# Four engines get orders of their own for the last five pairs of an attention pipeline, and two items' low parts move to VectorE

## What is computed

```
q, k, v = x @ Wq, ctx @ Wk, ctx @ Wv          # 16 heads of 64
logits  = q @ k^T * 64**-0.5 + column_bias
out     = softmax(logits) @ v                 # 128 x 1024
x       = out @ Wo + bo + x
```

## Time and profile before

| | |
|---|---|
| median of three runs | 1821.68 us |
| profiled execution: time / span | 1819.41 / 1816.8 us |
| TensorE matmul busy | 1757.9 us, 97% of the span |
| VectorE, ScalarE, GpSimd busy | 1579.0, 1471.8, 1599.6 us |
| mean granted TensorE clock | 0.978 |

### The profile page before, as it was taken

One profiled execution on the slowest core, in us unless ns is written; L12 is line 12 of the kernel. 1 busy time (PEld: TensorE's weight loads), 2 busy tenths in 40 slices (PEclk: granted clock), 3 DMA queues, 4 the chain that ended last, 5 costly groups with the idle time before them and its releaser, 6 DMA issues.

```text
span 1816.8 us, 72896 instructions
## 1 busy us (share of the span) xinstructions
PE 1757.9 (97%) x28400; PEld 1508.9 (83%) x28400; DVE 1579.0 (87%) x3010; ACT 1471.8 (81%) x2987; POOL 1599.6 (88%) x2136
## 2 busy tenths in 40 slices
PE   5599999999999999999999999999999999999996
PEld 5578888888888888888888888888888888888885
DVE  6689988899889998899888998899888898889983
ACT  3388888888888888888888888888888888888873
POOL 3389999999999999999999998999999999999983
PEclk7599999999999999999999999999999999999997
DMA  5269999999999999999999999999999999989996
GB/s 173 43 133 190 175 180 192 185 185 171 190 185 185 183 172 186 192 182 183 175 186 188 177 189 179 186 188 173 187 185 185 184 178 182 173 171 187 174 184 135
DMA packets 1168210, 320.35 MB, mean 176 GB/s; under 512 B 1140246, under 2 KB 1164124, under 8 KB 1167868
## 3 DMA queue, kind: packets, MB, share of 16 engines
q1 hardware_dynamic: 1167868, 315.69, 94.1%
HBM read 15.93 MB, written 4.19 MB: 11 GB/s over the span
## 4 chain that ended last, share of the span: by engine, by line
PE 90%; issue 1%; DMA 1%; SPq 1%; ACT 0%; DVE 0%; ACTq 0%; DVEq 0%
PE ring L1226 50%; PE sc L1368 12%; PE o_ps L1226 9%; PE o_ps L1386 5%; PE ring L1440 5%; PE sc L1347 4%; PE ring L1297 2%; PE sc L1366 1%; PE ring L1421 1%; PE ring L1437 1%; DMA arena<-p_sm 1%; PE ring L1274 0%; PE o_ps L1382 0%; PE ring L1277 0%; SPq L485 0%
## 5 line engine op out<-in xcount | busy, mean ns | idle before, releaser
L1226 PE MATMUL ring<-ctx_four,m_w 128*128 128x154 f16 x6144 | 461.5, 230 | 1.4 <-ACT o_tf L710 0.9
L1226 PEld LDWEIGHTS ring<-ctx_four,m_w 128*128 128x128 f16 x6144 | 429.1, 96 | 2.2 <-ACT o_tf L710 1.3
L1107 DVE TENSOR_TENSOR arena<-sc,row_max 128x616 f32<-128x616 f32 (+1 forms) x384 | 387.2, 1008 | 7.0
L644 POOL TENSOR_TENSOR p_sm<-arena,p_sm 128x616 f16<-128x616 f32 x256 | 334.5, 1318 | 39.4 <-ACT p_sm L710 38.0
L639 POOL TENSOR_TENSOR p_sg<-arena,p_sg 128x512 f16<-128x512 f32 (+1 forms) x256 | 342.0, 1358 | 2.3 <-ACT p_sg L710 2.3
L710 ACT ACTIVATE arena<-ring 128x462 f16<-128x462 f32 (+1 forms) x384 | 198.9, 518 | 153.8 <-PE ring L1226 153.4
L1086 DVE TENSOR_TENSOR arena<-ring,arena 128x462 f16<-128x462 f32 (+1 forms) x384 | 224.7, 586 | 73.0 <-ACT arena L710 64.1
L1226 PE MATMUL ring<-wv_m,ctx_four 128*103 128x512 f16 (+1 forms) x1152 | 281.1, 380 | 0.9 <-ACT v_all L710 0.9
L671 POOL TENSOR_TENSOR arena<-arena 128x1024 f16<-128x1024 f32 x128 | 272.8, 2131 | 8.8 <-ACT arena L710 8.8
L1368 PE MATMUL sc<-arena,x_s 128*128 128x512 f16 (+1 forms) x1152 | 263.6, 338 | 0.0
L1104 DVE TENSOR_REDUCE row_max<-sc 128x6 f32<-128x462 f32 (+2 forms) x384 | 211.1, 577 | 11.9 <-PE sc L1368 9.2
(11 more groups left out here) (172 smaller groups left out, 3720.8 us busy)
## 6 DMA issues: line engine op xcount, KB each, us to landing
v_fourth<-v_tile SPq DMA_DIRECT2D x64, 105.6 KB
ctx_nat<-in_ctx_dram SPq DMA_DIRECT2D x64, 77.0 KB
x_nat<-in_x_dram SPq DMA_DIRECT2D x64, 64.0 KB, 2.4
arena<-p_sg SPq DMA_TRANSPOSE x256, 3.8
arena<-p_sm SPq DMA_TRANSPOSE x256, 4.4
out_dram<-y_out SPq DMA_DIRECT2D x64, 64.0 KB, 2.2
v_fourth<-v_tile SPq DMA_DIRECT2D x32, 101.6 KB
arena<-in_L_xattn_Wk_dram SPq DMA_DIRECT2D x2, 1024.0 KB, 5.8
```

Of the source, the lines that this page charges most:

```text
L644: pool.tensor_tensor(p_sm[:, k, LO, :, 0:S], probs_m[:, hs, :], p_sm[:, k, HI, :, 0:S], ALU.subtract).then_inc(sems["pm_lo"], 1)
L1107: dve.tensor_tensor(out, s_view[:, hs, :], row_max[:, hs].unsqueeze(2).to_broadcast([P, hs.stop - hs.start, S]), ALU.subtract).then_inc(do ...
L1226: ins = pe.matmul(out, a, b, start=(n == 0), stop=(n == len(passes) - 1))
```

## The change

`pair` stays for everything up to the first pair of the tail. For tail pairs 1 to 5, SyncE, ScalarE, VectorE and TensorE get a `last_pair` of their own. GpSimd keeps `pair`, less the low parts of items 3 and 5 (`on_vector`), which VectorE now makes. In `output_m` of a last-layer item, the wait for `turned_o` moves behind the residual product; that holds for all 64 sequences. The pieces of the diff below belong, in this order, to the helpers, SyncE, GpSimd, ScalarE, VectorE and TensorE.

```diff
+    def on_vector(it, m):
+        return it == NIT and m >= 3
...
+            def last_pair(it, n):
+                m = 2 * n + 1
+                if n == 1:
+                    turn_m(it, m - 2, 1)
+                    turn_out(it, m - 4)
+                    store(it, m - 6)
+                if exists(it, m):
+                    turn_m(it, m, 0)
+                    turn_m(it, m, 1)
+                    if part(m) != 3:
+                        move_values(it, m)
+                if n > 1:
+                    if exists(it, m - 4):
+                        turn_out(it, m - 4)
+                    store(it, m - 6)
...
-                if exists(it, m - 4):
+                if exists(it, m - 4) and not on_vector(it, m - 4):
                     low_out(it, m - 4)
...
+            def last_pair(it, n):
+                g, m = 2 * n, 2 * n + 1
+                lead, chunks = fold_work(n)
...
+                if exists(it, m):
+                    exponential_m(it, m, 0)
+                    high_m(it, m, 0)
+                    exponential_m(it, m, 1)
+                if n > 1 and exists(it, m - 4):
+                    normalise_rest(it, n, m - 4)
+                if exists(it, m):
+                    high_m(it, m, 1)
+                if n > 1 and exists(it, m - 4):
+                    high_out(it, m - 4)
+                if n > 1:
+                    last_layer(it, n, m - 6)
+                for j, k in value_chunks(n):
+                    if exists(it, j):
+                        values(it, n, j, k)
...
+            def last_pair(it, n):
...
+                if n == 2:
+                    values(it, n - 1, *value_chunks(n - 1)[1])
+                if n > 1 and exists(it, m - 4):
+                    normalise_m(it, n, m - 4, 1)
+                if n == 1:
+                    normalise_m(it, n + 1, m - 2, 0)
+                if exists(it, m):
+                    low_part(it, m, 0)
+                    low_part(it, m, 1)
+                if exists(it, m - 4) and on_vector(it, m - 4):
+                    low_out(it, m - 4)
+                if n == 1:
+                    values(it, n, *value_chunks(n)[0])
+                if n > 1 and exists(it, m - 2):
+                    normalise_m(it, n + 1, m - 2, 0)
...
-                pe.wait_ge(sems["turned_o"], at("turned_o", it, m, 16))
...
                 pe.matmul(ring[:, b, 0:D], x_b[st][:, :], ident_y[:, :], start=True, stop=False)
+                pe.wait_ge(sems["turned_o"], at("turned_o", it, m, 16))
...
+            def last_pair(it, n):
+                g, m = 2 * n, 2 * n + 1
+                lead, chunks = fold_work(n)
+                if n == 2:
+                    for k in range(3):
+                        scores_m(it, m, k)
+                    context_values(it, n - 1, *value_chunks(n - 1)[1])
+                if exists(it, g - 4) or exists(it, m - 4):
+                    rest_and_turn(it, n, g - 4)
...
+                if n == 3:
+                    values_m(it, m - 2)
+                output_m(it, n, m - 6)
...
+                if n == 2:
+                    values_m(it, m - 2)
```

More of the change, by code:

```diff
@@ L555, in _ @@
                     pair(it, n)
-            for n in range(TAIL):
-                pair(NIT, n)
+            pair(NIT, 0)
+            for n in range(1, TAIL):
+                last_pair(NIT, n)
             for st in range(STREAMS):
@@ L693, in pair @@
                     x_parts(it, g + 4)
-                if exists(it, m):
+                if exists(it, m) and not on_vector(it, m):
                     low_part(it, m, 0)
@@ L910, in pair @@
                     normalise_rest(it, n + 1, m - 2)
+            def last_pair(it, n):
+                g, m = 2 * n, 2 * n + 1
+                lead, chunks = fold_work(n)
+                assert not exists(it, g - 2)
+                if exists(it, g - 4):
+                    turned(it, n, g - 4)
+                if exists(it, lead):
+                    folded(it, n, lead, chunks[0])
+                if n == 1:
+                    high_out(it, m - 4)
+                    last_layer(it, n, m - 6)
+                if exists(it, lead):
+                    folded(it, n, lead, chunks[1])
+                    folded(it, n, lead, chunks[2])
+                if exists(it, m):
[7 more added lines that the diff above has]
+                if n > 1 and exists(it, m - 4):
+                    high_out(it, m - 4)
+                if n > 1:
+                    last_layer(it, n, m - 6)
+                for j, k in value_chunks(n):
+                    if exists(it, j):
+                        values(it, n, j, k)
             for n in range(-3, PAIRS):
@@ L1209, in pair, with low_part, low_out @@
                         values(it, n, j, k)
+            def low_part(it, m, k):
+                hs = slice(k * HALF, (k + 1) * HALF)
+                dve.wait_ge(sems["pm_hi"], at("pm_hi", it, m, k + 1))
+                dve.tensor_tensor(p_sm[:, k, LO, :, 0:S], probs_m[:, hs, :], p_sm[:, k, HI, :, 0:S],
+                                  ALU.subtract).then_inc(sems["pm_lo"], 1)
+            def low_out(it, m):
+                dve.wait_ge(sems["o_hi"], at("o_hi", it, m, 1))
+                dve.tensor_tensor(o_s[:, LO, :], o_n, o_s[:, HI, :], ALU.subtract).then_inc(sems["o_lo"], 1)
+            def last_pair(it, n):
+                g, m = 2 * n, 2 * n + 1
+                lead, chunks = fold_work(n)
+                if exists(it, lead):
+                    for k in chunks:
+                        folded(it, n, lead, k)
+                if exists(it, g - 4):
+                    finish_g(it, n, g - 4)
+                if exists(it, m):
+                    maximum_m(it, m, 0)
+                    maximum_m(it, m, 1)
+                    shift_m(it, m, 0)
+                    maximum_m(it, m, 2)
+                    shift_m(it, m, 1)
+                if n == 2:
[4 more added lines that the diff above has]
+                    normalise_m(it, n + 1, m - 2, 0)
+                if exists(it, m):
+                    low_part(it, m, 0)
+                    low_part(it, m, 1)
+                if exists(it, m - 4) and on_vector(it, m - 4):
+                    low_out(it, m - 4)
+                if n == 1:
+                    values(it, n, *value_chunks(n)[0])
+                assert n == 1 or not any(exists(it, j) for j, k in value_chunks(n))
+                if n > 1 and exists(it, m - 2):
+                    normalise_m(it, n + 1, m - 2, 0)
             for n in range(-3, PAIRS):
@@ L1482, in pair @@
                         context_values(it, n, j, k)
+            def last_pair(it, n):
+                g, m = 2 * n, 2 * n + 1
+                lead, chunks = fold_work(n)
+                if n == 2:
[4 more added lines that the diff above has]
+                    rest_and_turn(it, n, g - 4)
+                if exists(it, lead):
+                    folded(it, n, lead, chunks[0])
+                if n == 3:
+                    values_m(it, m - 2)
+                output_m(it, n, m - 6)
+                if exists(it, lead):
+                    folded(it, n, lead, chunks[1])
+                    folded(it, n, lead, chunks[2])
+                if exists(it, g - 4):
+                    output_g(it, n, g - 4)
+                if n == 1:
+                    for k in range(3):
+                        scores_m(it, m, k)
+                    values_m(it, m - 2)
+                    context_values(it, n, *value_chunks(n)[0])
+                if n == 2:
+                    values_m(it, m - 2)
             for n in range(-3, PAIRS):
```

## The result

The changed kernel took 1824.12 us (median of 22 runs, 1822.31 to 1827.76) and the kernel before, on the same chip, 1819.7 us (22 runs): ratio 1.0025, 95% interval 1.0019 to 1.0031, slower by 4.4 us. The forecast ratio was 1.0027. The profiled execution has a span of 1820.9 us, 4.1 more than before.

The account below looks back on a forecast made before the run. TensorE was taken as busy 97% of the span, the tail as single file. X at 1795.0, 4.0 of SyncE issues, then landings and 2.96 us turns ended at 1821.8, +5.0; applied to the median, 1826.7 us, range 1821.5 to 1829.5.

Parts of the forecast that it names:

- VectorE's queue: VectorE's reordered list in tail pairs 1 and 2: its second values part frees item -1's ring bank at 1790.2, 5 us later.
- The low parts: Items 3 and 5 on VectorE: 0.75 us per 616-element low part, 1.24 per `low_out`, against 2.12 on GpSimd.
- X: Time when item 3's values are done on TensorE: forecast 1795.0, against 1793.7 before.
- SyncE's queue behind X: Item 5's two probability transposes go out before item 1's output transpose, which is issued at X + 4.0, 1799.0.
- The chain of output transposes: Items 1, 3 and 5 take turns on single `o_s` and `o_t`; last transpose at 1812.7, before 1807.20; span grows 5.0.
- its slack: On TensorE behind item 1's output product: item 5's rest over at about X + 11.5, `high_out(5)` only at X + 14.8.
- a sign that would turn the result: Item 5's second `p_sm` transpose ending in the chain, as in the earlier trace, would turn the forecast's sign.
- The reordering on ScalarE: ScalarE's new order in the tail lies beside the chain and costs and gives nothing.
- The short chain: Rival: same chain, TensorE's clock full, X = 1793.4, turns of 2.65; +2.0 us, 1823.7; chance 0.32.
- That item 5's values would set the end: Rival: item 5's halves issued without the store between, values setting the end; -1.4 to -3.0 us; chance 0.06.
- the main case: Chain of output transposes with item -1's product at the low clock: span +5.0, 1826.7 us; chance 0.56.
- The moved wait: In `output_m`: costs nothing before the tail, takes 0.54 us off the last output product in it.

Follow-up runs that it names:

- e1: Changed kernel with SyncE's transpose of item 1's output ahead of item 5's two probability transposes, TensorE's order unchanged; 1824.67 us, ratio 1.0024.
- e2: As e1, and TensorE's list also has item 1's output product ahead of item 5's values; 1819.86 us, ratio 1.0002.
- e4: Changed kernel with 60 added matmuls of 128 columns in TensorE's idle time before item -1's output product; 1820.95 us, ratio 1.0007.
- e9: Changed kernel with the changes of e2 and e4 together; 1820.25 us, ratio 1.0002.
- e5: Kernel before with only the wait for the turned output moved behind the residual product; 1818.27 us, ratio 0.9994.
- e3: Changed kernel with VectorE's second values part of item 3 ahead of item 5's maxima; 1822.12 us, ratio 1.0013.
- e7: Kernel before with e5 and e6 together, and SyncE's second half of item 5 right behind its first; 1817.27 us, ratio 0.9987.
- e6: Kernel before with only the low parts and output low parts of items 3 and 5 on VectorE, in old order; 1819.51 us, ratio 0.9999.
- e8: e7 with 36 added matmuls in TensorE's idle time between the last two output products; 1816.45 us, ratio 0.9981.

## Why the prediction was right

- **VectorE's queue.** The bank was to be free at 1790.2 and was at 1790.20. Counted from the fold block it came 0.5 earlier than I had it: two maxima took 1.26 where I had used 1.37, and the values part overlaps its neighbour. The low parts took 0.80 and 1.23 (counted: 0.75 and 1.24):

```profile
1784.30 1.54 DVE L1267 TENSOR_TENSOR p_sm<-arena,p_sm 128x616 f16<-128x616 f32 x2
...
1803.97 1.23 DVE L1273 TENSOR_TENSOR arena<-arena 128x1024 f16<-128x1024 f32 x1 [7.42 <-ACT arena L731]
```

The recorded remark that a `low_out` of 1.08 would take 0.3 off the sum is wrong: the sum goes by TensorE's 2.96 in both turns, which `low_out` doesn't enter.
- **X.** 1795.0 forecast, 1794.8 measured: the product at the low clock for most of its length (3.25), the values at the full one (1.31 behind the product's end). That the product would bring the full clock back held in this execution; with the same list up to there the 42 values matmuls took 1.98 in e1 and 2.49 in e2. e4 shows that the clock was 1.4 of it, and that without the low clock much of the loss goes.
- **SyncE's queue behind X.** 4.0 forecast, 3.98 measured (1794.80 to 1798.78). Two misses cancel in it: the first issue took 1.87 for 1.50, the second 1.59 for 2.0.
- **The chain of output transposes.** Forecast at 1799.0, 1806.0, 1812.7, measured 1798.78, 1805.73, 1811.97. The first turn took 6.95 (forecast 7.0). The second took 6.24 instead of 6.76: I had priced TensorE's product at the low clock, 2.96 from landing to issue, and it ran partly at the full one (1.97), so that ScalarE and VectorE set that turn, 2.6. This term was mis-sized by 0.4, with 0.2 in a landing (3.64 for 3.8). The end came at 1820.9 for 1821.8.
- **The step that the prediction left out.** In its sum item 1's product starts when item 1's transpose lands, at X + 8.0. The landing came there (1802.8), but TensorE's list has item 5's values ahead of that product, and the prediction placed them nowhere: its slack was for item 5's rest, behind the product. As the chain shows, the product stood behind item 5's second half, its matmuls (1801.14 to 1802.31) and its own residual (to 1802.90). The two ways ended 0.1 apart here, and 5.6 apart in e1. So the sum of this turn was right by a tie. The prediction had called that transpose on the chain a sign that would turn the result. It is on the chain, and the result didn't turn, since it leads to item 1's product and not, as in the earlier trace rows, to item 5's normalising.
- **The reordering on ScalarE**, put at nothing, cost nothing in the changed kernel: item 1's low part was over at 1795.0, and its transpose went out at 1798.78. In e2 and e9, where that transpose goes first, it is on the chain.
- **The rivals.** The short chain would have given X = 1793.4; neither the changed kernel nor e2 had it, e4 had to be given it. One term of that rival came true even so, its turn of 2.65 (the second turn, 2.60). That item 5's values would set the end needed an early `turn_out(1)`; e1 shows that even this isn't enough while TensorE's list has item 1's product behind those values.
- **What was luck.** Times from the start of the span agree better than the distances. The fold block stood at 1775.11 in the trace that the forecast was worked out from and at 1775.59 in the new one. Counted from it, the bank came after 14.6 us for 15.1, X after 19.2 for 19.9, the last output transpose after 36.4 for 37.6 and the end after 45.3 for 46.7. No stage was longer than forecast and several were shorter, and the growth of the tail, 3.6, lies half way between the main case (5.0) and the short one (2.0).
- **The moved wait** cost and gave nothing before the tail: after the change too, no idle time stands ahead of the 118 residual products before 1773 us, and e5's times don't differ from before.
- **The absolute time.** The forecast of 1826.7 stood on a median of three runs, 1821.68; over 22 runs the kernel before has 1819.7. The step of 5.0 measured 4.4 in the times and 3.6 in the tails of one execution each. The chances gave slower by over 0.2% only 0.55, for good reason: the lower end of the interval is 1.0019.

So the loss has two parts that hang together, each shown by changing it back or filling it: the order on SyncE and TensorE around item 1's output (e2, 4.1 us of the medians), and TensorE's gap with its low clock, made by VectorE's values part behind item 5's maxima (e4, 3.0; e3, 1.9). They are not additive (e9). The two parts that were free of the order, the moved wait and VectorE's low parts, are a small gain with the old order, together with item 5's second half ahead of the store (e7). The changed kernel's distance from e7 is 6.6 us, of which e2 and e9 win back about 4; the late `high_out` of item 1 on ScalarE is an untested candidate for the rest. What stays open too is why e4's medians fall by 1.2 more than its trace does.

## What to carry to other kernels

When a drain is reordered "by when data is ready", follow each single buffer (`o_s`, `o_t`) through every queue: a transfer that was pushed back by two places on one engine started a chain whose every turn costs a landing and a product, 6 to 7 us here, and putting it back on one engine alone gave nothing. A gap on TensorE can cost twice, once as a gap (3.45 us here) and once through the clock of what follows (1.4 us here); filler work of 60 small matmuls took off 3.0 of 4.4 us by the medians, 1.8 of 3.6 by the tails. And when the tail is 40 us of 1820, compare tails from a common row ahead of the change: in these traces that row starts anywhere from 1774.56 (e6) to 1776.41 (e9).

## What the runs showed that was not expected

The same 128x2048 transpose from SBUF to SBUF landed in 3.64 and 3.80 us in the changed kernel's last two turns, and in 5.3 us in e2 with no other transpose issued in the 3 us behind it (SyncE's next issue was at 1798.36, 3.3 later); in e9, with the same order, TensorE started on its landing 3.8 after the issue. The traces do tell the two apart. In e2 SyncE's issue itself took 3.11, in e9 1.61, and in e2 the data stop. From 1795 to 1799, in steps of 0.1 us:

```profile
GB/s 0 0 0 0 0 0 0 0 0 0 0 164 36 207 266 276 274 205 26 0 0 0 0 0 0 0 5 8 8 10 8 10 10 10 79 274 289 289 292 292
q8 instruction: 1, 0.02, 2.3%
```

For 1.5 us, from 1796.9 to 1798.4, next to nothing moves, and just ahead of the transpose's data a transfer of 0.02 MB ran on the queue that the profile lists as `instruction`. e9's transpose has neither the pause nor such a transfer. The 4.75 of item 5's second half in the kernel before has both: 0.02 MB at 1796.3, and at most 15 GB/s from 1796.9 to 1798.1. In e6 such a transfer ran too and the transpose landed in 3.84, so the transfer isn't shown to be the cause. Whatever it is, a single landing is uncertain by 1.5 us, a third of the whole effect. The kernel before's tail holds one such landing in its profiled execution: with the 3.83 of e7 in its place the tail would be 0.9 shorter and the growth 4.5 by this estimate, near the 4.4 of the medians.

And TensorE kept the full clock in e8 across an idle time of 2.89 us after a busy stretch, while after 3.45 us in the changed kernel it was at the low one for most of the next product. The idle time alone doesn't decide it. In e1 the same 2.89 stood ahead of a product that took 2.64:

```profile
1810.10 2.64 PE L1539 MATMUL ring<-wo_m,arena 128*128 128x128 f16 x24 [2.89 <-DMA arena<-arena]
```

There the granted clock had been 0.50 from 1800 to 1805 and 0.82 from 1805 to 1810, against 1.00 in both stretches in e8.
